# Copying gather indices for four groups at once on POOL, and writing scatter places on VectorE, in a graph network kernel

## The reference

```python
# layer 0, per edge
ef = jnp.concatenate([x[source], x[target]], axis=1)
h = jax.nn.leaky_relu(layer_norm(ef @ w1 + b1, g1, be1), SLOPE)
h = jax.nn.leaky_relu(layer_norm(h @ w2 + b2, g2, be2), SLOPE)
h = h * edge_attr[:, None]
out = jax.ops.segment_sum(h, target, num_segments=N)
# layer 3, per edge and head
scores = jnp.sum(q[src] * k[dest], axis=-1) / jnp.sqrt(jnp.float32(D))
scores = scores + attention_mask
# ... softmax over the edges of one source, weighted sum of v[src] into dest
```

## Time and profile before

| | us |
|---|---|
| median of 3 runs | 7370.18 |
| the runs, lowest to highest | 7369.54 to 7371.06 |
| the profiled execution | 7368.71 |
| its span in the profile | 7367.0 |

### The profile page before, as it was taken

How to read it: one execution, slowest core, us unless ns; L and a number is a source line. 1 busy time by engine, 2 the same in 40 slices (tenths; PEclk the granted TensorE clock), 3 DMA queues, 4 the chain that set the end, 5 groups by cost and what they waited for, 6 DMA issues and landing times. The chain is left out here.

```text
span 7367.0 us, 135158 instructions
## 1 busy us (share of the span) xinstructions
PE 4972.9 (68%) x26557; PEld 3915.5 (53%) x26558; DVE 4082.2 (55%) x13584; ACT 2784.0 (38%) x6869; POOL 4310.7 (59%) x5032
## 2 busy tenths in 40 slices
PE   3666666779666566986779566766666666415677
PEld 2555554458555465774557465544444444314555
DVE  4555557877323123664775123866666666553568
ACT  1555553237224235781342135931111111101259
POOL 3777771005677677007750776467777777537730
PEclk7777778999658558995899578977777777655789
DMA  1222223559546334883568356932222222213368
GB/s 30 73 73 73 73 73 120 184 191 383 186 128 193 89 96 126 307 279 87 158 190 264 92 165 212 299 118 69 69 67 69 67 69 67 64 36 82 109 198 291
DMA packets 560375, 1016.31 MB, mean 138 GB/s; under 512 B 118514, under 2 KB 127120, under 8 KB 559888
## 3 DMA queue, kind: packets, MB, share of 16 engines
q1 hardware_dynamic: 229424, 419.18, 17.6%
q10 hardware_dynamic: 197568, 359.75, 14.0%
q0 software_dynamic: 133280, 236.29, 12.9%
HBM read 624.60 MB, written 390.17 MB: 138 GB/s over the span
## 5 line engine op out<-in xcount | busy, mean ns | idle before, releaser
L448 PE MATMUL agg_bank<-agg_msgs,agg_onehot 128*128 x7840 | 1496.5, 351 | 706.7 <-DVE agg_onehot L386 572.5
L448 PEld LDWEIGHTS agg_bank<-agg_msgs,agg_onehot 128*128 128x128 f32 x7840 | 1287.8, 249 | 983.2 <-issue 979.1
L386 DVE TENSOR_TENSOR agg_onehot<-iota,rel 128x512 f32<-128x512 f32 x1176 | 814.9, 693 | 1418.6 <-SPq L354 734.8
L317 POOL DMA_INDIRECT agg_msgs<-y,agg_rows x784 | 779.3, 994 | 236.3 <-issue 195.6
L483 ACT ACTIVATE agg_kept<-agg_bank,inv_root 128x128 f32<-128x128 f32 x784 | 224.1, 368 | 708.5 <-PE agg_bank L448 687.8
L483 ACT ACTIVATE agg_kept<-agg_bank,inv_deg 128x128 f32<-128x128 f32 x784 | 224.1, 368 | 697.7 <-PE agg_bank L448 684.0
L448 PE MATMUL agg_bank<-agg_weighted,agg_onehot 128*128 x1568 | 336.6, 384 | 223.7 <-DVE agg_onehot L386 177.3
L1427 PE MATMUL score_pSrc<-ident,score_xs 128*128 128x128 f32 x392 | 154.9, 402 | 488.5 <-issue 357.4
L314 POOL DMA_INDIRECT agg_weight<-weights,agg_rows x392 | 413.5, 1055 | 121.4 <-issue 101.1
L1094 POOL DMA_INDIRECT mlp_xs<-in_x,mlp_rows x392 | 410.5, 1047 | 120.1 <-issue 119.1
L317 POOL DMA_INDIRECT agg_msgs<-near,agg_rows x392 | 388.0, 990 | 117.5 <-issue 96.9
(11 more groups left out here) (332 smaller groups left out, 12895.6 us busy)
## 6 DMA issues: line engine op xcount, KB each, us to landing
sums<-agg_kept ACTq DMA_DIRECT2D x490, 256.0 KB
agg_first<-y ACTq DMA_DIRECT2D x196, 256.0 KB
messages<-mlp_m SPq DMA_DIRECT2D x98, 256.0 KB, 2.1
agg_first<-in_x ACTq DMA_DIRECT2D x98, 256.0 KB
agg_msgs<-messages SPq DMA_DIRECT2D x98, 256.0 KB
l_z<-sums SPq DMA_DIRECT2D x98, 256.0 KB
x<-l_o POOLq DMA_DIRECT2D x98, 256.0 KB
near<-l_near_o SPq DMA_DIRECT2D x98, 256.0 KB
```

Source lines behind the costliest of these rows:

```text
L317: pool.indirect_dma_start(msgs[:, j, :], None, table[:, :], bass.IndirectOffsetOnAxis(ap=rows[:, third, j:j + 1], axis=0)).then_inc(sm[f"g ...
L386: nc.vector.tensor_tensor(onehot[:, j, :, :], k.iota[:, 0:P].unsqueeze(1).to_broadcast([P, Q, P]), k.rel[:, ds(i * (4 * Q) + j * Q, Q)].un ...
L448: t.matmul(bank[:, column[q], :], onehot[:, j, q, :], messages[:, slot[q], :], start=False, stop=True, skip_group_check=True)\
```

## The change

In both stages POOL copies the row numbers of four groups at once. `rows` becomes two halves of 2 x 16 columns; the copies of the next four groups' numbers (128x16, sources and targets) are issued in every fourth group, one after the second source gather and one after the second target gather; before them POOL waits for the landing of the gathers that read that half last. Between the fourth source gather and the first target gather nothing is left. The loops on POOL get a body of eight groups (`TWICE`), nine turns of it, and the last ten groups are laid out flat. A wait for `rows` stands only in every fourth group.

In the scores `copy_places` goes. DVE converts the places twice, once into `k.pos_i` and once into `places`, before the second after a wait that the scatter of group g-4 is through; `placed` is counted by the second, and POOL's scatter waits for `placed` directly.

The core of the diff (the perceptron's part; the scores' gather has the same edits):

```diff
 
 DEEP = 4
+TWICE = 2 * DEEP
 NODES_DEEP = 8
 
 
-def rounds(eng, body, lag=0, whole_numbers=2, deep=DEEP):
-
-    whole = GROUPS // deep
+def rounds(eng, body, lag=0, whole_numbers=2, deep=DEEP, last=0):
+
+    whole = GROUPS // deep - last
     for g in range(whole_numbers * deep):
         body(g // deep, g % deep)
...
-        rows = sb("rows", [P, DEEP, 2, Q], I32)
+        rows = sb("rows", [P, 2, 2, DEEP * Q], I32)
...
-                def copy_rows(g, u):
-                    nc.gpsimd.tensor_copy(rows[:, u, 0, :], k.src_row[:, ds(g * Q, Q)])
-                    nc.gpsimd.tensor_copy(rows[:, u, 1, :], k.dst_row[:, ds(g * Q, Q)]).then_inc(sm["rows"], 1)
-
-                copy_rows(0, 0)
-
-                def body(i, u):
-                    g = i * DEEP + u
-                    pool.wait_ge(sm["rows"], g + 1)
-                    if after(i, u, DEEP):
+                def copy_rows(g, half, which, groups):
+                    of = k.src_row if which == 0 else k.dst_row
+                    nc.gpsimd.tensor_copy(rows[:, half, which, 0:groups * Q], of[:, ds(g * Q, groups * Q)]).then_inc(sm["rows"], 1)
+
+                copy_rows(0, 0, 0, DEEP)
+                copy_rows(0, 0, 1, DEEP)
+
+                def body(i, u):
+                    g, b, times = i * TWICE + u, u % DEEP, i * 2 + u // DEEP
+                    half, at = u // DEEP, u % DEEP * Q
+                    if at == 0:
+                        pool.wait_ge(sm["rows"], times * 2 + 2)
+                    if after(i, u, DEEP, TWICE):
                         pool.wait_ge(sm["turned"], g - (DEEP - 1))
-                    pool.sem_inc(sm["pass_pool"], 1)
-                    for q in range(Q):
-                        pool.indirect_dma_start(xs[:, u, q, :], None, x[:, :], bass.IndirectOffsetOnAxis(
-                            ap=rows[:, u, 0, q:q + 1], axis=0)).then_inc(sm[f"src{u}"], 16)
-                    if not isinstance(i, int) or g + 1 < GROUPS:
-                        if after(i, u, DEEP - 1):
-                            was, place = before_by(i, u, DEEP - 1)
-                            pool.wait_ge(sm[f"src{place}"], was * (16 * Q) + 16 * Q)
-                            pool.wait_ge(sm[f"dst{place}"], was * (16 * Q) + 16 * Q)
+                    if at == 0 or after(i, u, DEEP, TWICE):
+                        pool.sem_inc(sm["pass_pool"], 1)
+                    to_copy = 0
+                    if u % DEEP == 2:
+                        to_copy = DEEP if not isinstance(i, int) else max(0, min(DEEP, GROUPS - (g + 2)))
+                        if to_copy and after(i, u, DEEP - 1, TWICE):
+                            was, place = before_by(i, u, DEEP - 1, TWICE)
+                            pool.wait_ge(sm[f"src{place % DEEP}"], (was * 2 + place // DEEP) * (16 * Q) + 16 * Q)
+                            pool.wait_ge(sm[f"dst{place % DEEP}"], (was * 2 + place // DEEP) * (16 * Q) + 16 * Q)
                             pool.sem_inc(sm["pass_pool"], 1)
-                        copy_rows(g + 1, (u + 1) % DEEP)
-                    for q in range(Q):
-                        pool.indirect_dma_start(xd[:, u, q, :], None, x[:, :], bass.IndirectOffsetOnAxis(
-                            ap=rows[:, u, 1, q:q + 1], axis=0)).then_inc(sm[f"dst{u}"], 16)
-
-                rounds(pool, body)
+                    for which, to, sem in ((0, xs, "src"), (1, xd, "dst")):
+                        for q in range(Q):
+                            pool.indirect_dma_start(to[:, b, q, :], None, x[:, :], bass.IndirectOffsetOnAxis(
+                                ap=rows[:, half, which, at + q:at + q + 1], axis=0)).then_inc(sm[f"{sem}{b}"], 16)
+                            if q == 1 and to_copy:
+                                copy_rows(g + 2, 1 - half, which, to_copy)
+
+                rounds(pool, body, deep=TWICE, last=1)
...
+                def scatter(i, u):
+                    g, b = i * TWICE + u, u % DEEP
+                    pool.wait_ge(sm["placed"], g + 1)
+                    pool.wait_ge(sm["scored"], g + 1)
                     pool.sem_inc(sm["pass_pool"], 1)
                     for q in range(Q):
...
-                def copy_places(i, u):
-                    if after(i, u, DEEP):
-                        pool.wait_ge(sm[f"scattered{u}"], i * (16 * Q))
-                    pool.wait_ge(sm["placed"], i * DEEP + u + 1)
-                    pool.sem_inc(sm["pass_pool"], 1)
-                    nc.gpsimd.tensor_copy(places[:, u, :], k.pos_i[:, ds((i * DEEP + u) * Q, Q)]).then_inc(sm["places"], 1)
-
-                def scatter(i, u):
-                    pool.wait_ge(sm["places"], i * DEEP + u + 1)
-                    pool.wait_ge(sm["scored"], i * DEEP + u + 1)
-                    pool.sem_inc(sm["pass_pool"], 1)
-                    for q in range(Q):
-                        pool.indirect_dma_start(by_source[:, :], bass.IndirectOffsetOnAxis(ap=places[:, u, q:q + 1], axis=0),
-                                                line[:, u, q, :], None).then_inc(sm[f"scattered{u}"], 16)
-
-                def body(i, u):
-                    for lag, step in ((0, gather), (2, copy_places), (3, scatter)):
-                        if live(*before_by(i, u, lag)):
-                            step(*before_by(i, u, lag))
-
-                copy_rows(0, 0)
-                rounds(pool, body, 3)
+                        pool.indirect_dma_start(by_source[:, :], bass.IndirectOffsetOnAxis(ap=places[:, b, q:q + 1], axis=0),
+                                                line[:, b, q, :], None).then_inc(sm[f"scattered{b}"], 16)
+
+                def body(i, u):
+                    for lag, step in ((0, gather), (3, scatter)):
+                        if live(*before_by(i, u, lag, TWICE), TWICE):
...
-                    v.tensor_copy(k.pos_i[:, ds(g * Q, Q)], pos_f[:, u % 2, :]).then_inc(sm["placed"], 1)
+                    v.tensor_copy(k.pos_i[:, ds(g * Q, Q)], pos_f[:, u % 2, :])
+                    if after(i, u, DEEP):
+                        dve.wait_ge(sm[f"scattered{u}"], i * (16 * Q))
+                    dve.sem_inc(sm["spread"], 1)
+                    v.tensor_copy(places[:, u, :], pos_f[:, u % 2, :]).then_inc(sm["placed"], 1)
```

## The result

The changed kernel takes 7319.39 us (median of 4 runs, 7309.7 to 7321.9) against 7369.86, a ratio of 0.9933 with a 95% interval of 0.9921 to 0.9945: 50 us, 0.67% faster. The forecast was 7328 us with a range of 7303 to 7352. The profiled execution took 7319.4 us, span 7317.8, so 49.2 us less than the span before.

The account below looks back on a forecast made before the run. POOL, issuing DMAs without a pause, was taken to bound both stages. Savings of 18.9 us (perceptron) and 43.8 (scores), less 14.4 for new copies and 6.5 for returning stretches, gave 41.8: 7370.2 to 7328 us, range 7303 to 7352.

Parts of the forecast that it names:

- What bounds the stages: Perceptron and scores: POOL issues its DMAs without a pause, so every microsecond of instructions between them lengthens the stage.
- the pairs: Row-number copies, two per group, between POOL's gathers: removal saves 18.9 us in the perceptron; in the scores 30.1 plus 2.4.
- the new copies: POOL, both stages: 96 copies of 16 columns, 48 per stage, add 0.15 us each, 14.4 us in all.
- The places: Scores: dropping POOL's copy of places saves 7.4 us of gaps and 3.9 us of longer scatters.
- cover of DVE's conversion: Scores: DVE's added 128x4 conversion hides in its idle time and costs nothing; uncovered it would cost 17 us.
- The rows of the scores: Scores: removing row-copy pairs saves 30.1 us plus 2.4 of longer gathers, before added wide copies and returning delays.
- returning stretches: Scores: half of the 13 us by which DVE lengthened copies reappears on POOL's DMAs, 6.5 us, bounds 0 and 13.
- (c): Scores: another engine becomes the limit, so only the perceptron gains, about 12 us, 7358 us; chance 0.03.
- (d): Both stages: POOL's ordinary gap hides the copies entirely, gain 0 to 5 us, 7368 us; chance 0.02.
- (e): POOL's loops of eight groups stall at 18 jumps back, 5 us each, 90 us slower, 7418 us; chance 0.03.
- (a): Both stages: stretches return in full and new copies meet DVE's busy moments, gain only 25 us, 7345 us; chance 0.18.
- (b): Both stages: stretched copies vanish, new ones are clean, DMAs slip past DVE; gain 63 us, 7307 us; chance 0.12.

Follow-up runs that it names:

- the part alone: Kernel before with only the perceptron's share of the change, edge_scores as before: 7349.38 us, 0.9982 of the kernel before on that chip.
- the second profile of the changed kernel: Changed kernel with nothing altered, run again on the chip where its three pieces were run separately: 7316.54 us, 0.9934 of the kernel before.
- the rows alone: Kernel before with only the scores' row copies made four groups at once, copy_places kept: 7337.57 us, 0.9961 of the kernel before.

## Why the prediction was right, point by point

**What bounds the stages** was read rightly: on the usual chips the gain of the whole is that of POOL's two stretches (50.2 against 49.2 us of span).

**The perceptron.** By the prediction 18.9 us for the pairs less 7.2 for the new copies, 11.7; measured 14.6 in the first profile, 15.4 in the part alone and 11.2 in the second profile of the changed kernel. In the first, the new copies were a little cheaper than 0.15 us: 1038.1 - 794.3 - 783 x 0.305 leaves 5.0 us for 48, 0.10 each, and 0.03 on the gather behind. The rest, 2 us, is less than the 4 us between the three profiles.

**The places.** 11.3 us by the prediction, 12.5 in the stage and 11.2 in time. The cover of DVE's conversion held; the 16 DMAs of the changed kernel that start while DVE is in the second one take 0.94 us.

**The rows of the scores.** This is the term that was mis-sized: 32.5 for the pairs, less 7.2 for new copies and less 6.5 for returning stretches, 18.8 us; measured 27.4 in the stage and 27.1 in time (19 to 39). The step that failed is "I count half of the 13 us of stretched copies as coming back": none did, as far as 5 us of scatter let one see. The new copies cost some 5.5 us instead of 7.2; what is left is within the scatter. In the kernel before, 43 of the 196 copies of rows start while DVE is in a product of line 1596 and hold 13 us of stretch. With the rows alone, 149 DMAs of the scores start in such a product instead of 115, but on average they last 1.09 us and no longer 1.14, so their stretch together is no larger. That the copies stood where DVE had most of the product still ahead of it (0.47 us on average, against 0.32 to 0.35 for the DMAs) is measured; that this is why nothing came back is argued.

**Sum.** 41.8 us forecast, 50.5 measured; a sixth too little, for that one term and the cheap copies. Rivals (c), (d) and (e) are refuted on the usual chips; (a) named the opposite of what happened with the stretches, (b) the right sign: 63 us against 50.5. The forecast of the whole was met in part by the width of its range: the stretches were taken to come back by half, and they came back by nothing.

## What to carry to other kernels

Where POOL issues indirect DMAs without a pause, a small copy between two of them costs 0.07 us for the first, 0.10 for a second and about 0.115 for each further one, and 16 columns cost the same as four: pool them, or give them to an engine with idle time, which by the medians brought another quarter of the change's gain. Price a POOL instruction by the gap it leaves, not by its duration, and look at where DVE's instructions with two SBUF operands fall: in the perceptron a gather started in the middle of one lasted longer by what was left of it less 0.1 to 0.15 us, and one started before it as a rule did not. An effect of half a per cent has to be read from the stage's first to last instruction: the rest of the kernel scattered by up to 15 us between executions.

## What the runs showed of the hardware that was not expected

- With four copies in a row instead of two the gathers around them were 6.5 us shorter in a stage of 1050, with the same work on DVE; nearly 5 us of difference occur between two profiles of one kernel.
- In the perceptron a gather lasted 1.25 us on average where it started during a DVE instruction with two SBUF operands, 0.94 where such an instruction began after it.
- One DVE instruction of 0.69 us per group cost POOL's stage 17.8 us over 98 groups, 0.18 each; the trace shows no wait for it, only longer DMAs.
- On one chip the same programs took 16% longer, with pauses of 3 to 15 us in which PE, DVE and ACT stood together. The time of one run there says nothing of the change; only the ratio to a run of the kernel before on the same chip does.
